# Joining two broadcast matmuls and moving layer-norm statistics one group later in an eight-core macaron block

## The reference

```python
def ffn(x, weight, disha):                    # weight (1024, 1024), disha (64, 1024)
    pooled = x.reshape(*x.shape[:-1], 16, 64).sum(axis=-2)
    return x @ weight.T + pooled @ disha

def attn(x):                                  # 16 heads of 64, latent 32
    q, k, v = heads(x @ c_attn_w.T)
    q, k, v = q @ q2l.T, k @ kv2l.T, v @ kv2l.T
    q, k = rope(q), rope(k)
    att = softmax(causal((q @ wqk.T) @ k.T * 32 ** -0.5))
    return merge((att @ v) @ l2o.T) @ cproj.T # biases left out here

x = x + 0.5 * ffn(layernorm(x), weight, disha)
x = x + attn(layernorm(x))
x = x + 0.5 * ffn(layernorm(x), weight, disha)
```

## Time and profile before

| | |
|---|---|
| median of two runs | 5660.04 us (5654.6 and 5665.48) |
| profiled execution | 5671.13 us |
| its span on the slowest core, core 1 | 5669.6 us |
| spans of the eight cores | 5621.8 to 5669.6 us |
| busy on core 1: PE, DVE, ACT, POOL | 3729.2, 1945.6, 1674.5, 698.8 us |
| mean granted clock of TensorE, by core | 0.720 to 0.742 |

### The profile page before, as it was taken

How to read it: one execution, slowest core, us unless ns; L and a number is a source line. 1 busy time by engine, 2 the same in 40 slices (tenths; PEclk the granted TensorE clock), 3 DMA queues, 4 the chain that set the end, 5 groups by cost and what they waited for, 6 DMA issues and landing times.

```text
span 5669.6 us, 58097 instructions; the slowest of 8 cores (5621.8 to 5669.6 us)
## 1 busy us (share of the span) xinstructions
PE 3729.2 (66%) x13322; PEld 1170.9 (21%) x13322; DVE 1945.6 (34%) x4078; ACT 1674.5 (30%) x1938; POOL 698.8 (12%) x884
## 2 busy tenths in 40 slices
PE   0116666677776766677776666677776666667777
PEld 0002212222221212122221221122222221222222
DVE  1115432531125433451123533353113543354123
ACT  0000350036620052005650035003770025102762
POOL 0002002200013101310003200320002200230001
PEclk9998658786677656776677765777777775788668
DMA  3242103210022101210003200320003210221002
GB/s 85 67 136 59 30 1 101 67 45 1 1 69 87 46 12 54 93 54 12 1 20 113 56 25 4 119 60 30 1 1 106 65 41 1 82 86 45 1 1 78
DMA packets 152515, 277.08 MB, mean 49 GB/s; under 512 B 34322, under 2 KB 34322, under 8 KB 152210
## 3 DMA queue, kind: packets, MB, share of 16 engines
q1 hardware_dynamic: 124818, 210.44, 12.9%
q0 software_dynamic: 8960, 29.37, 1.8%
q10 hardware_dynamic: 18432, 33.56, 1.6%
HBM read 231.36 MB, written 46.14 MB: 49 GB/s over the span
## 4 chain that ended last, share of the span: by engine, by line
PE 48%; DVE 16%; issue 15%; ACT 10%; DMA 5%; POOL 3%; SPq 1%; DVEq 1%; ACTq 0%; POOLq 0%
PE PS L904 12%; PE PS L865 10%; PE PS L620 8%; PE PS L690 7%; ACT PT L877 5%; PE PS L998 4%; DVE ln_sb L602 3%; DMA stg<-w_attn 3%; DVE rb_sb L950 3%; ACT r_sb L925 2%; DVE y_sb L955 1%; POOL sq_sb L558 1%; PE PS L568 1%; PE PS L563 1%; PE PS L799 1%
## 5 line engine op out<-in xcount | busy, mean ns | idle before, releaser
L877 ACT ACTIVATE PT<-PS,b_exp 128x1024 bf16<-128x1024 f32 (+7 forms) x1536 | 1257.1, 865 | 691.6 <-PE PS L865 661.3
L904 PE MATMUL PS<-PT,v_store 128*65 128x512 bf16 (+3 forms) x2560 | 904.1, 469 | 227.8 <-DVE y_sb L955 207.5
L865 PE MATMUL PS<-q_store,k_store 32*128 32x512 bf16 (+3 forms) x2560 | 770.9, 466 | 328.0 <-ACT PT L877 308.1
L620 PE MATMUL PS<-ln_sb,wslot 128*128 128x512 bf16 x2048 | 669.7, 469 | 162.0 <-DVE ln_sb L606 120.5
L883 DVE TENSOR_TENSOR PT<-PT,causal_sb 128x128 bf16<-128x128 bf16 x1024 | 230.2, 225 | 1482.0 <-ACT PT L877 1473.2
L690 PE MATMUL PS<-ln_sb,wslot 128*128 128x512 bf16 x2048 | 643.2, 462 | 82.4 <-DVE ln_sb L606 82.4
L555 POOL CAST xb_sb<-x_sb 128x512 bf16<-128x512 f32 x384 | 245.4, 639 | 3570.0 <-DVE x_sb L1008 2717.5
L575 ACT ACTIVATE m_bf<-PS 1x512 bf16<-1x512 f32 x48 | 28.2, 587 | 1856.2 <-PE PS L563 1823.5
L558 POOL TENSOR_TENSOR sq_sb<-xb_sb 128x512 bf16<-128x512 bf16 x384 | 398.4, 1037 | 887.9 <-PE PS L568 828.9
L904 PEld LDWEIGHTS PS<-PT,v_store 128*65 128x65 bf16 x2560 | 287.8, 134 | 760.5 <-issue 687.8
L865 PEld LDWEIGHTS PS<-q_store,k_store 32*128 32x128 bf16 x2560 | 180.0, 97 | 925.6 <-issue 904.2
(11 more groups left out here) (103 smaller groups left out, 2235.3 us busy)
## 6 DMA issues: line engine op xcount, KB each, us to landing
wslot<-me_strm SPq DMA_DIRECT2D x256, 256.0 KB, 2.7
wslot<-wa_strm SPq DMA_DIRECT2D x256, 256.0 KB, 2.6
wslot<-cp_strm SPq DMA_DIRECT2D x128, 256.0 KB, 2.7
out<-stg ACTq DMA_DIRECT2D x128, 256.0 KB, 3.1
x_sb<-x POOLq DMA_DIRECT2D x112, 256.0 KB, 4.3
stg<-w_attn SPq DMA_DIRECT2D x48, 256.0 KB
x_sb<-x SPq DMA_DIRECT2D x8, 512.0 KB
wa_strm<-build_sb SPq DMA_DIRECT2D x16, 256.0 KB
```

What stands on the lines that cost most here:

```text
L620: fns.append(lambda eng, j=j, dd=dd, bk=bk: eng.matmul(bank_ap(bk, 0, TTA), slot_ap(j, dd), ln_sb[:, TTA * dd:TTA * dd + TTA], start=(dd = ...
L865: hg=hg, gq=gq: eng.matmul(PS[:, 1024 * par + a:1024 * par + bnd], k_store[32 * hg:32 * hg + 32, seq * gq + 128 * c:seq * gq + 128 * c + 128],
L877: eng.activation(PT[:, QW * slot + qoff:QW * slot + QW], PS[:, 1024 * par + qoff:1024 * par + QW], AF.Exp, bias=b_exp[:, 0:1]),
L904: yb=yb: eng.matmul(PS[0:65, yb + a:yb + bnd], v_store[:, 1040 * c + 65 * h:1040 * c + 65 * h + 65], PT[:, QW * slot + a:QW * slot + bnd], ...
```

## The change

Two edits. In `ln_finish` the two broadcast matmuls become one group with one semaphore count; each still waits for its own input only. In the stages with spread statistics, chunk o - 3 follows group o from o = 3 on, and chunks 5, 6 and 7 follow the last group. `emit_cattn` is unchanged.

```diff
-        p.group("tensor", [lambda eng: eng.matmul(
-            bank_ap(6, 0, TTA), ones1x_sb[:], m_bf[:], start=True, stop=True)],
-            reads=[p.R("m_bf"), p.R("ones1x")], writes=[BK[6]])
-        p.group("tensor", [lambda eng: eng.matmul(
-            bank_ap(7, 0, TTA), ones1x_sb[:], a_bf[:], start=True, stop=True)],
-            reads=[p.R("a_bf"), p.R("ones1x")], writes=[BK[7]])
+        p.group("tensor", [
+            lambda eng: eng.matmul(bank_ap(6, 0, TTA), ones1x_sb[:], m_bf[:],
+                                   start=True, stop=True),
+            lambda eng: eng.matmul(bank_ap(7, 0, TTA), ones1x_sb[:], a_bf[:],
+                                   start=True, stop=True)],
+            reads=[p.R("ones1x")], writes=[BK[6], BK[7]],
+            fn_reads=[[p.R("m_bf")], [p.R("a_bf")]])
...
@@ emit_ffn
                 if nxt is not None:
-                    if tt == NT - 1 and o >= 2:
-                        ln_stats_chunk(0, o - 2, sqb=3)
+                    if tt == NT - 1 and o >= 3:
+                        ln_stats_chunk(0, o - 3, sqb=3)
...
-            if ln_next is not None and o >= 2:
-                ln_stats_chunk(ln_next, o - 2, sqb=lnbank)
+            if ln_next is not None and o >= 3:
+                ln_stats_chunk(ln_next, o - 3, sqb=lnbank)
         if ln_next is not None:
+            ln_stats_chunk(ln_next, 5, sqb=lnbank)
             ln_stats_chunk(ln_next, 6, sqb=lnbank)
             ln_stats_chunk(ln_next, 7, sqb=lnbank)
         if store and nxt is not None and tt == NT - 1:
+            ln_stats_chunk(0, 5, sqb=3)
             ln_stats_chunk(0, 6, sqb=3)
             ln_stats_chunk(0, 7, sqb=3)
...
@@ emit_cproj
-                if si == len(segs) - 1 and o >= 2:
-                    ln_stats_chunk(0, o - 2, sqb=2)
+                if si == len(segs) - 1 and o >= 3:
+                    ln_stats_chunk(0, o - 3, sqb=2)
             if si == len(segs) - 1:
+                ln_stats_chunk(0, 5, sqb=2)
                 ln_stats_chunk(0, 6, sqb=2)
                 ln_stats_chunk(0, 7, sqb=2)
```

## The result

The changed kernel took 5740.2 us (median of 11 runs, 5704.0 to 5764.5) against 5661.6 us for the kernel before (10 runs). The ratio is 1.013, 95% interval 1.010 to 1.016. So it is slower by 1.3%, where 0.2% was forecast, and above the range; only the forecast that it would stay within 2% came true. The profiled execution took 5736.7 us. The mean of the eight spans of the profiled executions went from 5643.9 to 5701.9 us (+58), the slowest from 5669.6 to 5735.1.

What follows compares the result with a forecast made beforehand. It took PE to hold 48% of the chain of waits, with attention's lines largest, and worked stage by stage: 28.7 + 8.1 + 3.2 + 1.0 - 28.7 - 0.7 = +11.6, giving 5672 us, range 5638 to 5705.

Steps and rivals of the forecast that it cites:

- Part 1: Joined broadcasts in `ln_finish`: the mb copy loses its cover, 0.61 us later in each of 47 places, +28.7 us.
- Rival (a): In `ln_finish`, the mb copy stays hidden and the joined broadcasts cost nothing: 5643 us; chance 0.07.
- cproj: Later statistics in cproj: chunk 6's square waits until behind group 7, 1.01 us later in 8 stages, +8.1 us.
- FFN1: Later statistics in FFN1: the last cast comes 0.20 us later in each of 16 stages, +3.2 us.
- a pair costs PE some 0.45: Sizing from cproj: a chunk's two statistics matmuls add 0.45 us between group starts, 2.36 against a 1.90 group.
- FFN2 of tile 0: With prefetch, five POOL-queue stalls become four, saving 5.9 us against 1.82 more at the end: -4.1, x7 = -28.7 us.
- FFN2 of tile 1: With prefetch, one stall of 1.72 us saved against 1.82 for one more chunk: -0.1 a stage, x7 = -0.7 us.
- three such stalls become two: In FFN2 of tile 1 with prefetch, stalls of 1.72 us remain only behind groups 3 and 5.
- rival (b): FFN2's dense starts wait for stores with two output tiles: 6.4 us in 14 stages, 90 more, 5761 us; chance 0.07.
- Rival (c): In FFN2 of tile 0 the stall only moves and nothing is saved: 41 us more, 5713 us; chance 0.06.
- Attention: Unedited second halves fall by luck into either of two patterns, 25 us to either side: 5647 or 5697; chance 0.13.
- Rival (e): In FFN2 of tile 0 the dense start keeps the high clock two groups longer: 23 us less, 5649; chance 0.07.

Runs made afterwards that it cites:

- e1: Kernel before with only the joined broadcast group, statistics staying behind group o+2: 5696.7 against 5650.5 us, ratio 1.0074.
- e2: Kernel before with only the statistics one group later, broadcasts kept in two groups: 5676.2 us, ratio 1.0039.
- e6: Changed kernel with four output tiles in place of two: 5697.2 us, ratio 1.0060 to the kernel before.
- e9: Kernel before with statistics ahead of the prefetch DMA in FFN2 of tile 0, plus four output tiles: 5484.7 us, ratio 0.9679.
- e3: Kernel before with five unused DVE multiplications delaying attention by 2.5 us in each half: 5743.6 us, ratio 1.0140.
- e4: Kernel before with seven unused DVE multiplications delaying attention by 3.6 us in each half: 5689.7 us, ratio 1.0052.
- e8: Kernel before with statistics ahead of the prefetch DMA in POOL's queue in FFN2 of tile 0: 5479.8 us, ratio 0.9690.
- e10: The changed kernel run again, unaltered, for a second profile: 5747.8 us, ratio 1.0164 to the kernel before.

## Why the prediction was wrong, step by step

**Part 1 held in its stages.** 0.61 us was foretold for each `ln_finish` and 0.5 to 0.7 was measured in the mean of each kind of stage, 0.60 in the median of nearly all, with the mb and ab copies back to back. Rival (a) is out. The kernel with this edit alone is slower by some 20 us more than that, by its mean span (e1), and where they lie stays open. The Trainium skill (TensorE: Matmul & The Clock Gate, The cost: per-tile semaphore tail) favours one count on the last matmul of a pack, since counts take time one after the other. No run here shows a gain from it: the first matmul's reader was made to wait for the second, and the rows show only the 0.60 lost.

**cproj held.** +1.01 was foretold, +0.99 measured, in part by luck; the tail from the last x update to L575 went from 1.35 to 2.87 us. The timeline of its end, changed kernel, against the earlier trace rows:

```profile
2229.97 0.38 PE L568 MATMUL PS<-sq_sb,ones_sb 128*1 128x512 bf16 x1
...
2230.50 1.04 POOL L558 TENSOR_TENSOR sq_sb<-xb_sb 128x512 bf16<-128x512 bf16 x1 [0.76 <-PE PS L568]
2231.48 0.61 POOL L555 CAST xb_sb<-x_sb 128x512 bf16<-128x512 f32 x1
...
2232.35 0.38 PE L563 MATMUL PS<-xb_sb,ones_sb 128*1 128x512 bf16 x1 [0.18 <-PE PS L568]
```

Foretold were 2229.93, 2230.46, 2231.44 and 2232.30. That the moments themselves agree is chance, since the two runs come to this stage at different times; what counts are the distances from one to the next, and these are as foretold. The square of chunk 6 stands behind group 7, as said. But the interval without statistics is shorter by 0.63 us here too, and not by the 0.45 that the sum has, so this step alone would give 0.83.

**FFN1 was mis-sized.** +0.20 was foretold, nothing came (the interval between the adds of groups 2 and 3 fell from 2.36 to 1.73 us, the tail rose from 2.16 to 2.81). The term that failed is "a pair costs PE some 0.45". That was 2.36 less the 1.90 of a group's span by modelled ends; from start to start a group without a pair takes 1.73, so a pair costs 0.63. With it the step gives 0.02 in place of 0.20, and the sum loses 3.2.

**FFN2 of tile 0, the step held, its size less so.** One interval of five went, the four others stayed at 8.04 to 8.28, and the tail grew by 1.80 (6.98 to 8.78) against 1.82 foretold. But "saved: 5.9" was 8.30 - 2.4. The interval that went is that between groups 2 and 3, 7.69 in the mean and the shortest of the five (7.13 in the earlier trace rows itself, 2250.37 to 2257.50), and its successor took 2.83, because nearly all of these adds meet a store (41 of the 42 in the complete records, 30 in e2). That is 4.9, and 5.5 in e2. With the tail it leaves -3.1 and not -4.1 a stage, some 7 us of the miss in seven stages; the last half's tile 0, without prefetch, gave 1.3 us of it back. I had the 7.13 in the rows and took the 8.30 of its neighbours.

**FFN2 of tile 1, the step failed.** It said "three such stalls become two", the first one gone for nothing, with -0.1 a stage as the net. Measured is +2.25 beside part 1's 0.60. The five intervals between the adds of groups 2 and 7 sum to 18.2 us before and to 18.2 after: nothing was saved, the 1.83 of the tail were paid, and the other 0.4 lie in the groups ahead. What failed first is the count of stalls. By PE's group starts three long intervals are left, and the first of them has only moved from behind group 2 to behind group 3, with two output tiles and with four; without any store wait the five intervals gain 0.7 us where 1.72 stood in the sum, and the stage loses 1.0 net of part 1 (42.56 - 0.60 against 40.93, e6 and e9). The rest, 0.8 to 1.2 a stage, is rival (b): without a pair the third add comes so early that its output tile, that of two groups before, is still being stored. I gave (b) 0.07 because in the six other stages the adds kept step with PE. That reading was wrong: on core 1 two of the six held their adds behind the matmuls for 0.9 and 4.3 us, and on the six cores with complete records 30 of 42 stages did so for over 0.5 us before, and all 42 after; the mean went from 1.7 to 3.7 us of such delay a stage. Where the adds did keep step, the statistics paused PE; this pause is what the edit takes away. The price that (b) had, 6.4 us a stage, was too high: DVE is idle for 6.38 us in the earlier trace rows, but group 3's matmuls run for most of that,

```profile
983.46 1.89 PE L620 MATMUL PS<-ln_sb,wslot 128*128 128x512 bf16 x8
```

and the store holds the add of 988.13 for some 2.5 us. Rival (c), that the stall only moves, was named for tile 0, where it didn't come; tile 1, where it came, wasn't asked.

**Attention, the step failed in kind.** The prediction saw the two patterns, 499.11 and 474.24 us, and took them for luck without a sign, with a chance of 0.13. In two profiles the changed kernel has long attentions more often (7 short ones of 32 both times, against 17 and 20), and they are worth +25 on the mean of the cores in the first pair of profiles and +41 in the second. e3 and e4 show that a delay alone, with all of the rest as before, brings the mean to 380.6 or to 364.4 us. With the counts by sequence, which return with the kernel, that rules out mere chance: the stretch depends on the moment at which it begins, and an edit that moves that by 1 to 3 us has a cost or a gain there of up to 50 us. That it is the place in the pattern of the clock's changes which decides is argued and not shown; the rows show that long ones have the lower granted clock. How the loss divides between the edits isn't settled: each alone moves single sequences both ways. The sum of their ratios, 1.0113, lies within the interval of the first comparison of both (1.010 to 1.016). I know of no way to foretell the sign from the trace of before.

**Rival (e)** didn't come: with four stalls left, the saved interval brought nothing beyond itself. What it named, the low clock behind the stalls, shows in e8, where the stalls are short and the granted clock of groups 3 to 7 is 0.90.

The terms together, in the mean of a core: part 1 as foretold, FFN1 -3.8, cproj -0.2, FFN2 of tile 0 +5.4, FFN2 of tile 1 +17.9, attention +25.0 and -1.2, the qkv stages +2.8. With 12.3, the forecast column's sum (it counts 48 `ln_finish`), that is the 58.2 between the two first profiles. The mean span of all twelve runs of the changed kernel is 5704.0 us, and that of the kernel before 5627 to 5636 in its four sets of runs, so the usual difference is 68 to 77 us, and 80.5 in e10's own group; what is beyond 58 is in large part attention, by the second pair of profiles.

## What to carry to other kernels

Before a stall is counted as removed, follow the queue that makes it: here POOL reached the first chunk as late as before, and the stall stood one group later. Ask also what the pause has been hiding: here it gave the stores time, and without it the next add waited for them instead. Put compute that others wait for ahead of a DMA in an engine's queue when that DMA has to wait for a third engine; this order was worth 3.1%, where moving the work by a group was worth nothing. And judge an edit of a few us by its stages, with a second kernel that has a bare delay in it, when a long stretch elsewhere takes different times for the same work.

## What the runs showed of the hardware that I had not expected

- The same attention work, with the same instruction counts and DVE and ACT times, takes 359 to 388 us at a granted clock of 0.73 to 0.61, by when it starts. A delay of 2.5 us in each half cost the kernel 1.4%, one of 3.6 us 0.5%. In one kernel all eight cores took the short time in one sequence and none in another (e1).
- In that regime added work can be harmless: the changed kernel with some 8 us of added DVE operations ran at 1.0107 of the kernel before, without them at 1.013 and 1.0164.
- Two output tiles are too few when groups come 1.7 us apart: DVE stood idle up to 4.8 us (core 4) before an add, until a store ended whose landing takes 3.1 us in the median. Four tiles took all of these waits away.
- A whole stage of 8 groups went from 65.8 to 40.5 us by the order of POOL's queue alone, and its granted clock from 0.65 to 0.78.
